# Sparse second feed-forward: small rings for a pair's weights and targets, x buffer released by transposes and copies, weight splits regrouped

## The reference, cut to what matters

```
scores = sigmoid(x @ gate_w.T)                  # 4096 tokens, 16 experts
pick 2 of 4 groups, then the best 4 experts; weights = chosen scores, normed, * 2.5
g, u   = x @ gate_proj[e].T, x @ up_proj[e].T   # 256 -> 128, each expert
y      = sum over the 4 chosen e of weight * ((silu(g) * u) @ down_proj[e].T)
y     += the same with one shared expert, for every token
out    = x + tanh(g_ffn[1]) * y                 # x normed before the layer
```

## Time and profile before

| | |
|---|---|
| median of 3 runs | 1696.85 us |
| the profiled execution: its time, its span | 1699.63 us, 1697.9 us |
| busy over the span: PE, DVE, ACT, POOL | 73%, 55%, 46%, 31% |
| DMA moved | 181.32 MB, mean 107 GB/s |
| granted TensorE clock, mean | 0.852 |
| `moe` | from 1085 us on, 613 of the 1698 us |

### The profile page before, as it was taken

How to read it: one execution, slowest core, us unless ns; L and a number is a source line. 1 busy time by engine, 2 the same in 40 slices (tenths; PEclk the granted TensorE clock), 3 DMA queues, 4 the chain that set the end, 5 groups by cost and what they waited for, 6 DMA issues and landing times. The chain is left out here.

```text
span 1697.9 us, 27596 instructions
## 1 busy us (share of the span) xinstructions
PE 1238.2 (73%) x9252; PEld 1134.9 (67%) x9252; DVE 931.1 (55%) x2022; ACT 788.0 (46%) x2121; POOL 518.6 (31%) x581
## 2 busy tenths in 40 slices
PE   3775129995899999999999998547765666666563
PEld 2554028984788888888888887447665665666553
DVE  5885925551766665776677777545622222224445
ACT  3554125552556676656565665434333333333331
POOL 4341263641000010004520454141344555233331
PEclk8666559997999999999999999777877878787887
DMA  3459824545000000002310233364345543335666
GB/s 96 132 163 215 199 98 123 160 101 133 8 7 12 4 20 26 8 1 88 119 57 2 88 125 107 105 203 137 94 125 151 155 133 112 92 94 170 200 204 202
DMA packets 140575, 181.32 MB, mean 107 GB/s; under 512 B 22528, under 2 KB 120992, under 8 KB 139936
## 3 DMA queue, kind: packets, MB, share of 16 engines
q1 hardware_dynamic: 113072, 127.90, 26.1%
q0 software_dynamic: 17792, 43.14, 8.0%
q10 hardware_dynamic: 9584, 8.60, 1.8%
HBM read 111.51 MB, written 72.32 MB: 108 GB/s over the span
## 5 line engine op out<-in xcount | busy, mean ns | idle before, releaser
L2236 POOL DMA_INDIRECT answers<-moe_yb,moe_xg x160 | 156.5, 978 | 302.1 <-ACT moe_yb L2301 262.5
L1591 ACT ACTIVATE attend_s<-attend_s,attend_less 128x128 f32<-128x128 f32 x512 | 198.3, 391 | 107.7 <-DVE attend_less L1732 97.4
L2465 PE MATMUL moe_psX<-const_ident,moe_xg 128*128 128x128 f32 x384 | 78.3, 339 | 172.9 <-DMA moe_xg<-slots 141.4
L2465 PEld LDWEIGHTS moe_psX<-const_ident,moe_xg 128*128 128x128 f32 x384 | 54.4, 173 | 184.1 <-DMA moe_xg<-slots 150.4
L1546 POOL TENSOR_TENSOR router_xn<-rest_acc,router_mv 128x512 f32<-128x512 f32 x12 | 12.5, 1045 | 443.3 <-DVE router_rs L1234 387.1
L1202 POOL DMA_INDIRECT slots<-router_row,router_idx x96 | 98.1, 1022 | 105.4 <-DMA router_row<-normed_rows 82.3
L2284 ACT ACTIVATE moe_xh<-moe_psX 128x512 fp32r<-128x512 f32 x96 | 57.4, 598 | 150.8 <-PE moe_psX L2465 144.2
L81 PE MATMUL moe_psU<-moe_wh,moe_xl 128*128 (+1 forms) x384 | 125.9, 328 | 0.0
L2355 DVE TENSOR_TENSOR moe_it<-moe_it,moe_psU 128x256 f32<-128x256 f32 x96 | 40.2, 419 | 155.9 <-ACT moe_it L2292 121.1
L82 PE MATMUL moe_psU<-moe_wl,moe_xh 128*128 (+1 forms) x384 | 122.9, 320 | 0.0
L83 PE MATMUL moe_psU<-moe_wh,moe_xh 128*128 (+1 forms) x384 | 121.4, 316 | 0.0
(11 more groups left out here) (368 smaller groups left out, 4192.1 us busy)
## 6 DMA issues: line engine op xcount, KB each, us to landing
moe_xg<-slots SPq DMA_DIRECT2D x160, 129.0 KB
moe_yt<-answers SPq DMA_DIRECT2D x32, 512.0 KB
router_row<-normed_rows SPq DMA_DIRECT2D x48, 256.0 KB
layer_raw<-in_wi_dram SPq DMA_DIRECT2D x8, 1024.0 KB, 5.2
layer_raw<-in_wo_dram SPq DMA_DIRECT2D x8, 1024.0 KB, 6.8
moe_raw<-in_gex_dram SPq DMA_DIRECT2D x17, 384.0 KB, 3.8
slots<-fill SPq DMA_DIRECT2D x32, 129.0 KB
mix_xin<-in_x_dram SPq DMA_DIRECT2D x8, 512.0 KB, 3.9
```

The costliest lines, as they stand in the source:

```text
L1591: last = nc.scalar.activation(s[:, g, j, :], s[:, g, j, :], ACT.Exp, bias=less[:, g, j:j + 1], accum_out=sm[:, g, j:j + 1])
L2236: nc.gpsimd.indirect_dma_start(out=R.YT[q], out_offset=bass.IndirectOffsetOnAxis(ap=xg[:, j % NX, s, D + 1:D + 2].bitcast(I32), axis=0), i ...
L2465: last = nc.tensor.transpose(psX[j % 2][:, k * N + s * P:k * N + (s + 1) * P], xg[:, j % NX, s, k * P:(k + 1) * P], C["ident"][:])
```

## The change: what it does

- Two rings of 8 pairs are added, `wd` (weights, float) and `dst` (targets, int). DVE's new `targets(j)` copies the two columns of a routed pair out of `xg` in iteration j-2, with a wait for the scatters of the pair 8 before. `y_out` and `scatter` read the rings.
- `load(j)` waits for the transposes of pair j-6 (`t_done`) and, if that was routed, for its two copies (`d_up`).
- `raw` has 3 slots and `yt` 2, so that all fits; `row` shares its memory with `yt` as before.
- The low half of every fourth weight (3, 7, 11, 15) is made by POOL, the other 13 by DVE. Before POOL had the 8 odd ones.
- SP's `load_row` steps stand 4 later in j; `answers` begin at step 78 instead of 75 and go 4 for every 3 steps instead of 8 for every 7; the combines begin at iteration 74 instead of 72.

```diff
-    NX, NY, NR, NT, NS = 6, 5, 2, 3, 4
+    NX, NY, NR, NT, NS, NM = 6, 5, 3, 2, 4, 8
+        wd, dst = sb("wd", [P, NM, 2]), sb("dst", [P, NM, 2], I32)
...
+        def fourth(k):
+            return k % 4 == 3
+
         def split(eng, k):
 
-            if k % 2:
-                eng.wait_ge(w_odd, k // 2 + 1)
+            if fourth(k):
+                eng.wait_ge(w_fourth, k // 4 + 1)
             else:
-                eng.wait_ge(w_even, k // 2 + 1)
+                eng.wait_ge(w_most, k + 1 - (k + 1) // 4)
...
-        answered_from = STARTS_OF[1] + NX + 1
+        answered_from = STARTS_OF[1] + NX + 4
         asked_at, combined_at = {}, {}
         for k in range(PART_B[0]):
-            asked_at.setdefault(answered_from + k * 7 // 8, []).append(k)
-            combined_at.setdefault(answered_from + k * 7 // 8 - 3, []).append(k)
+            asked_at.setdefault(answered_from + k * 3 // 4, []).append(k)
+            combined_at.setdefault(answered_from + k * 3 // 4 - 4, []).append(k)
...
                 if j >= NX:
-                    if is_shared(j - NX):
-                        sp.wait_ge(t_done, j - NX + 1)
-                    else:
-                        scattered(sp, NTH[j - NX])
+                    sp.wait_ge(t_done, j - NX + 1)
+                    if not is_shared(j - NX):
+                        sp.wait_ge(d_up, NTH[j - NX] + 1)
...
             weights(1)
+            weights(2)
...
-                h = j - sends_from - 1
+                h = j - sends_from - 5
...
-                    nc.gpsimd.indirect_dma_start(out=R.YT[q], out_offset=bass.IndirectOffsetOnAxis(ap=xg[:, j % NX, s, D + 1:D + 2].bitcast(I32), axis=0),
+                    nc.gpsimd.indirect_dma_start(out=R.YT[q], out_offset=bass.IndirectOffsetOnAxis(ap=dst[:, r % NM, s:s + 1], axis=0),
...
             for t in range(4):
                 R.send(pool, LAST - 1, t)
-                low(4 * t + 1)
                 low(4 * t + 3)
...
+                act.wait_ge(d_up, r + 1)
...
-                    last = nc.scalar.activation(yb[:, r % NY, s, :], psY[j % 2][:, s * D:(s + 1) * D], ACT.Copy, scale=xg[:, j % NX, s, D:D + 1])
+                    last = nc.scalar.activation(yb[:, r % NY, s, :], psY[j % 2][:, s * D:(s + 1) * D], ACT.Copy, scale=wd[:, r % NM, s:s + 1])
...
+            def targets(j):
+
+                r = NTH[j]
+                dve.wait_ge(x_in[j % NX], x_count(j))
+                if r >= NM:
+                    scattered(dve, r - NM)
+                v.tensor_copy(wd[:, r % NM, :], xg[:, j % NX, :, D])
+                v.tensor_copy(dst[:, r % NM, :], xg[:, j % NX, :, D + 1].bitcast(I32)).then_inc(d_up, 1)
...
                     x_low(j + 2)
+                    if not is_shared(j + 2):
+                        targets(j + 2)
...
-                if 2 * j + 2 < EXPERTS:
-                    low(2 * j + 2)
+                for k in (2 * j + 1, 2 * j + 2):
+                    if k < EXPERTS and not fourth(k):
+                        low(k)
```

More of the change, by code:

```diff
@@ L2005, in moe @@
         raw = sb("raw", [P, NR, PER])
-        yt = sb("yt", [P, NT, TOP * D])
-        row = yt[:].rearrange("p a n -> p (a n)")[:, 0:NS * 2 * WIDE].rearrange("p (h a n) -> p h a n", h=NS, a=2)
+        both = sb("both", [P, max(NT * TOP * D, NS * 2 * WIDE)])
+        yt = both[:, 0:NT * TOP * D].rearrange("p (a n) -> p a n", a=NT)
+        row = both[:, 0:NS * 2 * WIDE].rearrange("p (h a n) -> p h a n", h=NS, a=2)
         cnt, need, ends = (sb(n, [P, E1]) for n in ("cnt", "need", "ends"))
@@ L2025, in moe @@
         sent = [sem(f"sent{k}") for k in range(NS)]
-        w_hi, w_even, w_odd, t_done, x_hi, x_lo, u_done, s_up, i_up, i_done, i_hi, i_lo, y_done, y_up = (
-            sem(n) for n in ("w_hi", "w_even", "w_odd", "t_done", "x_hi", "x_lo", "u_done", "s_up", "i_up", "i_done", "i_hi", "i_lo", "y_done", "y_up"))
+        w_hi, w_most, w_fourth, t_done, x_hi, x_lo, u_done, s_up, i_up, i_done, i_hi, i_lo, y_done, y_up, d_up = (
+            sem(n) for n in ("w_hi", "w_most", "w_fourth", "t_done", "x_hi", "x_lo", "u_done", "s_up", "i_up", "i_done", "i_hi", "i_lo", "y_done", "y_up", "d_up"))
         made, r_done, r_free, col_up, table_up, pad_in, marked, c_up, c_step, stored, added = (
@@ L2228, in low @@
                 r = place_w(k)
-                nc.gpsimd.tensor_tensor(wl[:, r], raw[:, k % NR, :], wh[:, r], ALU.subtract).then_inc(w_odd, 1)
+                nc.gpsimd.tensor_tensor(wl[:, r], raw[:, k % NR, :], wh[:, r], ALU.subtract).then_inc(w_fourth, 1)
             def scatter(j):
@@ L2342, in low @@
                 r = place_w(k)
-                v.tensor_tensor(wl[:, r], raw[:, k % NR, :], wh[:, r], ALU.subtract).then_inc(w_even, 1)
+                v.tensor_tensor(wl[:, r], raw[:, k % NR, :], wh[:, r], ALU.subtract).then_inc(w_most, 1)
             def x_low(j):
```

## The result

The changed kernel takes 1511.68 us (median of 4 runs, 1509.3 to 1517.75), the kernel before 1697.62 us in its own 4 runs (1689.47 to 1701.12). The ratio is 0.8916, with a 95% interval of 0.8875 to 0.8958: 186 us less. The forecast was 1544 us with a range of 1508 to 1600, so direction and range held, and the gain was 33 us larger than the sum made it.

What follows compares the result with a forecast made beforehand. A loop from `y_out` through scatters, SP's loads and PE's transposes was taken as the bound. Terms -16 -13 -57 -52 -22 +7 = -153 from 1699.63 gave 1546.6, so 1544 us after 2.8 for the median; range 1508 to 1600.

Steps and rivals of the forecast that it cites:

- The loop: From `y_out` through scatters, their landing, SP's load and PE's transposes to a later `y_out`; claimed to set pairs 22 to 90.
- B: Pairs 22 to 53: loads come early, POOL bounds at 4.05 us per pair; -57 us, bounds -25 and -61.
- C: Pairs 54 to 71, no sends: 2.9 us per pair plus 4 us for backlog; -52 us, bounds -35 and -56.
- D: Pairs 72 to 90: two answer slots and DMA nearly equal bounds, 5.25 us per iteration; -22 us, bounds -10 and -32.
- the rival with all terms near their good bounds: Whole kernel: every stage gains close to its most favourable bound, about 1522 us; chance 0.12.
- W: Start of the stretch, first steps: row loads about 15 us apart instead of 20.4; -16 us, bounds -7 and -20.
- A: Pairs 12 to 21: without waits for loads DVE bounds, 47 us in all; -13 us, bounds -6 and -16.
- T: Tail, last eight answers with two slots instead of three: about 37 us from 30.8; +7 us, bounds +3 and +10.
- The period that was given as a sign: Pairs 22 to 53 after the change: 4.0 to 4.4 us, with POOL's instructions over 85% of the time.
- Copies: DVE's new copies lie in its idle half and cost POOL 0.1 us per pair; bounds nothing or 2 x 0.5 us.
- the rival built on them: Slower: copies hold up POOL's scatters; 1760 us at 3 us, about 1825 by the skill's figure; chance 0.03.
- The clock: Rival: PE's clock stays low in half of the pairs 22 to 71, +39 us, 1583 us; chance 0.15.

Runs made afterwards that it cites:

- release_late: release_only with the copies of weights and targets moved behind `i_low` in DVE's order: 1506.85 us, ratio 0.8907 to the kernel before.
- slots_3: The changed kernel with three answer slots and two slots of raw weights, as before the change: 1500.97 us, ratio 0.8859 to the kernel before.
- release_only: The kernel before plus only the two rings, their copies and the earlier release of the x buffers: 1568.48 us, ratio 0.9225.
- copies_x4: The changed kernel with six further small copies per routed pair on DVE, ahead of `i_low`: 1584.59 us, ratio 0.9304 to the kernel before.

## Why the prediction was right, and where its sizes were off

**The loop.** Right. PE's wait for loads went from 141.4 to 3.7 us, B, C and D shortened by 160 us together, and release_late shows that the release carries it: with none of the regrouping it comes to 1507 us, beside 1512 for the whole change.

**The number.** It was closer to a miss than it looks. 1511.68 us lie 3.7 us inside the lower end of the range, outside the forecast's own part of it (1520 to 1572) and below the rival with all terms near their good bounds (1522). B and D went beyond their good bounds of -61 and -32 us.

**The terms**, profiled execution against profiled execution. Forecast -153, measured 1512.18 - 1699.63 = -187.5:

| term | forecast | measured |
|---|---|---|
| W, start to silu of pair 12 | -16 | -15.6 |
| A | -13 | -14.1 |
| B | -57 | -76.7 |
| C | -52 | -50.6 |
| D | -22 | -33.2 |
| T | +7 | +2.8 |

**W and A** held. Of W's 15.6 us, 1.5 were there before silu of pair 0, where the third weight was to cost 1.2. The row loads came 16 to 17 us apart, not 15. A was worked out as 47 us and took 47.6; its -13 comes from the edge 1.3 us too late, and with 61.7 us for the stage before it is -15.

**B** is the step that failed, by 20 us: "POOL is next: 32 x 4.05 = 130, and 4 to fill the ring". POOL's period was right (3.97). The stage, though, is cut at `y_out`, and the rings let `y_out` run ahead of POOL before it must keep POOL's pace. The first 12 pairs take 35.8 us, 2.98 each, PE's own pace at a clock of 1.00; the other 20 take 78.8, 3.94 each. Filling the ring doesn't cost 4 us, it saves 12 x (4.05 - 2.98) = 12.8; with the 4 that fall away and 20 x 0.11 for the period this is 19 of the 20. POOL's instructions fill 77% of the stage, not over 85%: its gaps of 0.30 us between issues are not counted as busy, as the earlier trace rows already showed. The period that was given as a sign, 4.0 to 4.4, is 3.6 over the stage for the same reason.

**C** held: 3.22 per pair at a clock of 1.00, with POOL's backlog worked off, where 2.9 and 4 us besides were forecast.

**D** was 11 us too long. The slot cycle is the bound, as forecast, but it was rounded up twice. 21 intervals between combines take 74.56 us, 3.55 each, not 3.75; by that an iteration is 4.73, and the stage took 4.59, where 5.25 was taken from two "nearly equal bounds". These are the first and the last combine of the 22, in DVE's timeline of the changed kernel:

```profile
1398.11 0.69 DVE L2425 TENSOR_TENSOR moe_both<-moe_both 128x512 f32<-128x512 f32 x1 [3.07 <-DMA moe_both<-answers]
...
1472.67 0.69 DVE L2425 TENSOR_TENSOR moe_both<-moe_both 128x512 f32<-128x512 f32 x1
```

That three slots bring D to 69.8 us at a DMA share of 0.93 shows that DMA wasn't the second of two equal bounds; at that share 19 iterations took 3.67 each. What the prediction took for DMA's need (4.1 to 4.5) came from a share times a length, and that isn't a need: in slots_3 the same product is 3.4 us per iteration.

**T** went the same way. Its start and end are as counted, 5.4 us to the issue of the first answers and 2.2 after the last combine; the four cycles of the two slots take 26 us, 6.5 each, instead of 30, so 33.6 in all instead of 37.

**Copies.** Costing them at near nothing on POOL was right, and the rival built on them fell: the median of the scatters is 962 ns with two copies per pair, 961 with eight. The prediction had also carried over 3.1 us per scatter from the Trainium skill (SBUF — State Buffer, "SBUF: two separate sides"). The same section says that a DMA of GpSimd's is blocked until the copy on DVE ends and about 115 ns more; by it copies of 0.16 us can hold up a scatter by about 0.3 us (an estimate from that page), not by 2.5. Not even that is seen: in the changed kernel 50 of the 160 scatters overlap one of the two copies, with a median of 962 ns and a maximum of 984. But "in its idle half" missed their real risk. It lies not in their busy time, 0.16 us each, but in their place ahead of `i_low`, on the chain that PE waits for.

**The clock.** "The rings let PE run without gaps" held for the changed kernel. It was nearer to failing than the chance of 0.15 says: three neighbours of this kernel fell into the slow round. That the changed kernel isn't in it was not foreseen by any step of the prediction; in this part it was luck.

**Open.** Why the copies' place decides in release_only, where they add only 0.14 us ahead of `i_low` (on DVE's timeline the first starts at 1290.46 and `i_low` at 1290.60), isn't settled; that moving them ends the round is shown in three pairs of kernels, the reason is argued. Nor is it settled what holds PE's signals back in the round, or why the changed kernel, with the copies ahead, stays out of it. A changed kernel whose slow round is started by a stand of PE alone was not tried.

## What to carry to other kernels

Free a buffer when its last large reader is done, and copy the few words that a late reader needs into a small ring. Then put that copy in the engine's order behind whatever the bound engine waits for, not where its operand happens to be ready: in three neighbours of this kernel its place cost 60 us where its duration cost none. When consumers of an engine start microseconds after the ends that the profile records for it, don't read its idle time as a cause. When a stage is bound by one engine and cut at another, count the rings between them as time won, and when an idle-looking slot is traded for another, price both sides by the slot's cycle: here three slots of each, paid with one y buffer, gave 1491 us.

## What the hardware showed that was not expected

- A stage can settle into a round of two pairs, 10.5 us in copies_x4, with one recorded stand of TensorE of about 3.1 us in it. The 5.1 to 5.3 us per pair are the price of a pair in a stretch mostly at half clock, 5.18 in the earlier trace rows, though half of the recorded products show the full clock.
- In that round TensorE's signals come up to several us after the recorded ends of its instructions (2.1 and 3.6 us in the lines above) and in bursts of four and more within 0.6 us. The work between four signals in a row takes longer than a burst: at full clock in the changed kernel they lie 1.4 us apart, first to last. Whether the records run ahead or the signals are held back, no run settles; ACT and DVE start by the signals.
- The DMA engines moved 334 GB/s in D of slots_3, more than the 309 of the start in the earlier trace rows; with two slots the same stage moved 274.
